# TensorE's program of 20 expert jobs written out in place of a loop over 10 pairs of jobs

## The chip, the cores and the metric

The kernel runs on one core of one Trainium2 chip. The metric is the device time of one execution in microseconds (us). Each engine of the core has a program of its own, and the engines keep in step by semaphores. PE is TensorE, DVE is VectorE, ACT is ScalarE, POOL is GpSimd, SP is SyncE, which here only issues transfers.

## The reference, cut to what matters

The reference is one transformer layer over 1024 tokens (32 sequences of 32) of width 512: cross attention, self attention, and then a mixture of experts with 8 experts, of which each token takes the best two:

```
logits = (x @ gate_w + gate_b) / TEMP
topk_vals, topk_idx = jax.lax.top_k(logits, TOP_K)
...
h = jnp.einsum('bsd,edf->bsef', x, w1) + b1
h = jax.nn.gelu(h, approximate=False)
expert_out = jnp.einsum('bsef,efd->bsed', h, w2) + b2
out = jnp.einsum('bse,bsed->bsd', gate_probs, expert_out)
```

followed by a layer norm and the residual. `w1` is 512 x 2048 and `w2` 2048 x 512 for each expert. The change lies in this last stage.

## The kernel before, in words

**Stages.** The first 780 us or so are the two attentions and the routing. The routing sorts the 2048 (token, expert) pairs by expert and cuts them into `JOBS` = 23 jobs of 128 rows each; a job belongs to one expert, and `job_e` holds each job's expert, which is known only at run time. From 786 us to 1303 us TensorE works on the jobs, and a short tail gathers the rows and normalizes them.

**A job on TensorE.** `job(j, turn)` (line 804) reads the job's expert `e` from memory into a register (`value_load`, line 805). Its work is in quarters of the 2048 hidden columns, `fb` = 0 to 3:

- `mm1(j, turn, fb, e)` (line 775): 48 matmuls of 128 columns in fp16, in 16 triples (lines 787, 788, 789). Numbers are kept as a high and a low half, so that a product takes three matmuls. The weights lie in one of two slots, chosen by `e % 2`; so the address of each piece of weights is worked out in a register, on TensorE's own sequencer, just before the instruction that uses it: two such steps a triple. These stay after the change, since `e` stays unknown.
- `mm2(j, fb)` (line 792): 12 matmuls of 512 columns (lines 799, 800, 801), with fixed addresses.
- `xt_fill(j + 1)` (line 765): four transposes (line 770) of the next job's rows.

They are interleaved as `mm1(j,0), mm2(j-1,2), mm1(j,1), xt_fill(j+1), mm2(j-1,3), mm1(j,2), mm2(j,0), mm1(j,3), mm2(j,1)`. Each `mm1` waits for a count of `h_act` (and the first for `xt_out` and `experts_in`), each `mm2` for `hT_out` and `v_low_done`, `xt_fill` for `xs_in` and `xt_out`. A count is a formula in `j`, such as

```
pe.wait_ge(hT_out, FB * j + fb + 1)
...
pe.wait_ge(v_low_done, 2 * (FB * j + fb + 1))
```

With `j` a Python number, that is a constant in the wait; with `j` a loop's register, it is worked out by a register step first.

**Loops.** Jobs 0, 1 and 22 are written out, in TensorE's program as in this text's diff. Jobs 2 to 21 are a hardware loop (`Fori`, line 828) of 10 passes over two jobs, since `turn` alternates. ACT and DVE run their own part of each job (gelu at line 490, the halves of `w2` at lines 506 and 647, the halves of the hidden rows at lines 498 and 638) in loops of their own; SP loads the next expert's 8 MB (lines 385 and 387) when `mm2_done` shows that a slot is free; POOL gathers rows and adds results (lines 433 and 438).

**Program code.** Each engine's instructions are fetched from the chip's memory by transfers that the profile lists under the kind "instruction", by queue.

Of the kernel before, what the change touches and what calls it, by code (L numbers as in the profile page):

```python
# [55 lines left out]
JOBS = TOKENS * TOPK // P + EXPERTS - 1  # L56
# [38 lines left out]
def perceiver_layer(nc, x, ctx_768, g_x, b_x, g_c, b_c, Wq, Wk, Wv, Wo, W_qkv, W_o,  # L95
                    gate_w, gate_b, w1, b1, w2, b2, ln_g, ln_b, out):
    with ExitStack() as stack:
# [666 lines left out]
        def moe_pe(pe):  # L764
            def xt_fill(j):
                pe.wait_ge(xs_in, 16 * (j + 1))
                if not isinstance(j, int) or j > 0:
                    pe.wait_ge(xt_out, j)
                for c in range(KD):
                    last = nc.tensor.transpose(XT[c], xs[:, c * P:(c + 1) * P], ident[:, :])  # L770
                    if c == 0 and isinstance(j, int) and j == 0:
                        last.then_inc(mm2_done, 1)
                last.then_inc(xt_full, 1)

            def mm1(j, turn, fb, e):
                if fb == 0:
                    pe.wait_ge(xt_out, j + 1)
                    pe.wait_ge(experts_in, e * 48 + 48)
                if not isinstance(j, int) or j > 0:
                    pe.wait_ge(h_act, FB * (j - 1) + fb + 1)  # L780
                elif fb == 2:
                    pe.wait_ge(b1_cols_ok, 1)
                for c in range(4):
                    into = bank[fb][:, c * P:(c + 1) * P]
                    for k in range(KD):
                        high, low = [moe_flat16[:, bass.ds((e % 2) * 32768 + (2 * k + i) * FF + fb * 512 + c * P, P)] for i in range(2)]
                        nc.tensor.matmul(into, high, xT_low[turn][:, k, :], start=(k == 0), stop=False)  # L787
                        nc.tensor.matmul(into, high, xT_high[turn][:, k, :], start=False, stop=False)  # L788
                        last = nc.tensor.matmul(into, low, xT_high[turn][:, k, :], start=False, stop=(k == KD - 1))  # L789
                last.then_inc(h_full, 1)  # L790

            def mm2(j, fb):
                pe.wait_ge(hT_out, FB * j + fb + 1)
                if fb == 0 and (not isinstance(j, int) or j > 0):
                    pe.wait_ge(ys_raw, j)
                pe.wait_ge(v_low_done, 2 * (FB * j + fb + 1))
                for c in range(4):
                    high, low = [v_place(part, j, fb, c // 2)[:, (c % 2) * DIM:(c % 2 + 1) * DIM] for part in range(2)]
                    nc.tensor.matmul(Y[:, :], hT_low[:, fb % 2, c, :], high, start=(fb == 0 and c == 0), stop=False)  # L799
                    nc.tensor.matmul(Y[:, :], hT_high[:, fb % 2, c, :], high, start=False, stop=False)  # L800
                    last = nc.tensor.matmul(Y[:, :], hT_high[:, fb % 2, c, :], low, start=False, stop=(fb == 3 and c == 3))  # L801
                last.then_inc(mm2_done, 1)

            def job(j, turn, first=False, last=False, behind=True):
                e = 0 if first else pe.value_load(job_e[0:1, bass.ds(j, 1)], min_val=0, max_val=EXPERTS - 1)
                mm1(j, turn, 0, e)
                if not first:
                    mm2(j - 1, 2 if behind else 3)
                mm1(j, turn, 1, e)
                if not first and not last:  # L810
                    xt_fill(j + 1)
                if behind:
                    mm2(j - 1, 3)
                mm1(j, turn, 2, e)
                mm2(j, 0)
                mm1(j, turn, 3, e)
                mm2(j, 1)
                if first:
                    xt_fill(j + 1)
                    mm2(j, 2)  # L820
# [4 lines left out]
            job(0, 0, first=True, behind=False)  # L825
            pe.wait_ge(jobs_ready, 1)
            job(1, 1, behind=False)
            with pe.Fori(2, JOBS - 1, 2) as j:
                job(j, 0)
                job(j + 1, 1)  # L830
            job(JOBS - 1, 0, last=True)
            mm2(JOBS - 1, 2)
            mm2(JOBS - 1, 3)
# [844 lines left out]
        def _(pe):  # L1678
# [347 lines left out]
            body(GROUPS - 1, True, True, False)  # L2026
            body(GROUPS, False, True, False)
            moe_pe(pe)


# [21 lines left out]
```

## Time and profile before

| what | value |
|---|---|
| median of 3 runs | 1328.2 us (1325.65 to 1328.8) |
| the profiled execution's own time | 1326.96 us |
| its span, first to last instruction | 1325.3 us |
| TensorE clock granted, mean | 0.993 |
| PE busy | 1277.7 us, 96% of the span |
| DVE busy | 971.1 us, 73% |
| ACT busy | 963.9 us, 73% |
| POOL busy | 219.1 us, 17% |

The busy time of PE overlaps itself, since matmuls are pipelined: a 128-column matmul is shown with 220 ns, while the next one starts 56 ns later. So the length of a stretch is read from the starts of its instructions, not from busy time. Register steps, branches and waits are run by an engine's sequencer and are not counted as busy; the view of a source line lists them under PEldq for TensorE.

### The profile page before, as it was taken

The page shows a single profiled execution, that of the slowest core. Times are in us where ns is not written, and L with a number is a line of the kernel's source. Part 1 is how long each engine was busy: PE and PEld are TensorE (multiplying, and loading weights), DVE is VectorE, ACT ScalarE, POOL GpSimd, SP SyncE. Part 2 cuts the span into 40 slices and gives each one's busy share as a digit, 9 for nine tenths or more (in the row PEclk, how much of TensorE's full clock was granted, in tenths as well). Part 3 has the DMA queues.
Part 4 walks back from the last instruction along what each step waited for, and adds up shares of the span by engine and source line. Part 5 has one row for each costly group of instructions (what it writes and reads, how often), then busy time and mean ns, then how long its engine had stood idle before and what let it go on. Part 6 is the DMA issues. An engine that isn't in the chain of part 4 may idle for free.

```text
span 1325.3 us, 34868 instructions
## 1 busy us (share of the span) xinstructions
PE 1277.7 (96%) x11476; PEld 952.9 (72%) x11477; DVE 971.1 (73%) x2140; ACT 963.9 (73%) x1741; POOL 219.1 (17%) x270
## 2 busy tenths in 40 slices
PE   7999999999999999999999789999999999999997
PEld 7768768677697696786876666777777777777773
DVE  5775878877877878788766757776767676767677
ACT  3577776776777777776877537787888888888784
POOL 1001002012030120030210213121212121111112
PEclk9999999999999999999999889999999999999999
DMA  9527246154363372552732895546262626710104
GB/s 365 191 101 255 90 159 223 63 209 169 99 252 122 110 250 87 182 198 68 255 146 90 317 344 166 222 168 201 95 214 80 228 79 229 277 32 16 32 9 135
DMA packets 69838, 216.36 MB, mean 163 GB/s; under 512 B 5582, under 2 KB 5820, under 8 KB 64652
## 3 DMA queue, kind: packets, MB, share of 16 engines
q1 hardware_dynamic: 63568, 201.71, 42.0%
q0 software_dynamic: 6192, 13.98, 5.1%
q8 instruction: 31, 0.51, 0.1%
q14 instruction: 19, 0.16, 0.0%
q10 hardware_dynamic: 28, 0.01, 0.0%
HBM read 169.46 MB, written 46.22 MB: 163 GB/s over the span
## 4 chain that ended last, share of the span: by engine, by line
PE 67%; DMA 9%; issue 8%; DVE 7%; ACT 4%; POOL 3%; SPq 1%; DVEq 0%; POOLq 0%; ACTq 0%
PE bank L799 7%; PE bank L1755 7%; PE bank L787 6%; PE bank L789 6%; PE bank L801 6%; PE bank L800 6%; PE bank L788 6%; DMA w_halves<-arena 4%; DMA w_halves<-moe_w 3%; PE bank L1804 3%; PE bank L1789 3%; PE bank L1821 3%; PE bank L1792 2%; PE bank L1764 2%; PE bank L1889 2%
## 5 line engine op out<-in xcount | busy, mean ns | idle before, releaser
L787 PE MATMUL bank<-arena,moe_w 128*128 128x128 f16 x1472 | 256.2, 220 | 0.9 <-DVE arena L630 0.9
L789 PE MATMUL bank<-arena,moe_w 128*128 128x128 f16 x1472 | 256.4, 220 | 0.0
L788 PE MATMUL bank<-arena,moe_w 128*128 128x128 f16 x1472 | 255.6, 219 | 0.0
L1755 PE MATMUL bank<-moe_w 128*128 128x257 f32 x768 | 188.6, 383 | 0.0
L787 PEld LDWEIGHTS bank<-arena,moe_w 128*128 (+1 forms) x1472 | 143.8, 98 | 14.9 <-DVE arena L630 1.2
L788 PEld LDWEIGHTS bank<-arena,moe_w 128*128 (+1 forms) x1472 | 144.1, 98 | 10.3
L1755 PEld LDWEIGHTS bank<-moe_w 128*128 128x128 f32 x768 | 137.9, 190 | 17.7
L789 PEld LDWEIGHTS bank<-arena,moe_w 128*128 (+1 forms) x1472 | 143.8, 98 | 1.5 <-issue 0.2
L490 ACT ACTIVATE arena<-bank,now_act 128x128 f32<-128x128 f32 x368 | 136.8, 449 | 7.9 <-PE bank L789 4.5
L506 ACT ACTIVATE wosT<-moe_w,now_act 128x1024 f16 (+1 forms) x90 | 98.5, 1143 | 37.7 <-PE bank L801 37.7
L1147 ACT ACTIVATE moe_w<-bank,cols,ugain 128x512 f32<-128x512 f32 x96 | 74.4, 776 | 59.7 <-PE bank L1805 58.7
L438 POOL DMA_INDIRECT acc_rows<-arena,job_idx x22 | 52.1, 2368 | 396.3 <-DVE arena L671 396.3
L1377 DVE TENSOR_TENSOR moe_w<-bank,moe_w 128x512 f16<-128x512 f32 (+1 forms) x96 | 65.4, 689 | 48.1 <-ACT moe_w L1161 45.8
L647 DVE SCALAR_TENSOR_TENSOR arena<-moe_w,now_v,wosT 128x1024 f16<-128x1024 f16 (+1 forms) x45 | 57.8, 1285 | 52.5 <-ACT wosT L506 50.3
L647 DVE SCALAR_TENSOR_TENSOR kqT<-moe_w,now_v,y 128x1024 f16<-128x1024 f16 (+1 forms) x45 | 57.8, 1285 | 51.3 <-ACT y L506 51.0
L1009 POOL TENSOR_TENSOR crstd<-cmv,half 128x3 f32<-128x3 f32 x32 | 28.7, 898 | 396.1 <-DVE cmv L1334 396.1
L1161 ACT CAST moe_w<-bank 128x512 f16<-128x512 f32 (+1 forms) x96 | 54.3, 585 | 47.2 <-PE bank L1779 46.9
L506 ACT ACTIVATE y<-moe_w,now_act 128x1024 f16 (+1 forms) x45 | 51.7, 1149 | 43.5 <-PE bank L801 43.5
L1789 PE MATMUL bank<-moe_w 128*128 128x512 f16 x192 | 73.0, 380 | 3.7 <-DVE moe_w L1377 1.8
L1792 PE MATMUL bank<-moe_w,arena 128*128 128x512 f16 x192 | 72.6, 378 | 0.0
L1140 ACT ACTIVATE moe_w<-bank,negm 128x257 f32<-128x257 f32 x128 | 59.0, 467 | 15.9 <-DVE negm L1357 15.3
L638 DVE SCALAR_TENSOR_TENSOR arena<-arena,now_h 128x512 f16<-128x512 f32 x92 | 68.7, 746 | 1.6 <-ACT arena L498 1.6
(296 smaller groups left out, 3099.3 us busy)
## 6 DMA issues: line engine op xcount, KB each, us to landing
moe_w<-in_L_ffn_w_dram SPq DMA_DIRECT2D x46, 1024.0 KB, 6.4
moe_w<-w_halves SPq DMA_DIRECT2D x8, 4096.0 KB
moe_w<-in_L_ffn_w_dram SPq DMA_DIRECT2D x8, 4096.0 KB
w_halves<-moe_w SPq DMA_DIRECT2D x48, 512.0 KB, 4.2
arena<-in_ctx_dram SPq DMA_DIRECT2D x32, 384.0 KB
arena<-in_L_ffn_w_dram SPq DMA_DIRECT2D x10, 1024.0 KB, 4.9
blocks<-in_L_ffn_w_dram SPq DMA_DIRECT2D x8, 1024.0 KB, 4.8
w_halves<-arena SPq DMA_DIRECT2D x8, 512.0 KB
```

The source lines that it names most:

```text
L490: last = nc.scalar.activation(h_sb[:, fb % 2, c * P:(c + 1) * P], bank[fb][:, c * P:(c + 1) * P], ACT.Gelu, bias=now_act[:, 4 + 4 * fb + c ...
L506: nc.scalar.activation(v_place(0, j, fb, i), moe_flat[:, bass.ds(slot * 16384 + 8192 + fb * 2048 + i * 1024, 1024)], ACT.Identity, scale=n ...
L647: nc.vector.scalar_tensor_tensor(out=v_place(1, j, fb, i), in0=moe_flat[:, bass.ds(slot * 16384 + 8192 + fb * 2048 + i * 1024, 1024)], sca ...
L787: nc.tensor.matmul(into, high, xT_low[turn][:, k, :], start=(k == 0), stop=False)
L788: nc.tensor.matmul(into, high, xT_high[turn][:, k, :], start=False, stop=False)
L789: last = nc.tensor.matmul(into, low, xT_high[turn][:, k, :], start=False, stop=(k == KD - 1))
L799: nc.tensor.matmul(Y[:, :], hT_low[:, fb % 2, c, :], high, start=(fb == 0 and c == 0), stop=False)
L800: nc.tensor.matmul(Y[:, :], hT_high[:, fb % 2, c, :], high, start=False, stop=False)
L801: last = nc.tensor.matmul(Y[:, :], hT_high[:, fb % 2, c, :], low, start=False, stop=(fb == 3 and c == 3))
L1755: last = nc.tensor.matmul(bank[h][:, 0:KEYS], qkT[:, c, b, h * P:(h + 1) * P], cnT[:, b % 2, c, :], start=(c == 0), stop=(c == KC - 1))
L1789: nc.tensor.matmul(ps[:, :], n_high[:, b % 2, k, columns], pT_high[:, k, :], start=(k == 0), stop=False)
L1792: nc.tensor.matmul(ps[:, :], n_low[:, b, k, columns], pT_high[:, k, :], start=False, stop=False)
```

## The change

The loop of TensorE's expert jobs becomes a Python loop, so that each of the jobs 2 to 21 is written out with its number as a constant. The order of the matmuls, their operands and all that is waited for stay. `turn` is `j % 2`, which is what the loop had. The programs of the other engines are not touched.

```
             job(1, 1, behind=False)
-            with pe.Fori(2, JOBS - 1, 2) as j:
-                job(j, 0)
-                job(j + 1, 1)
+            for j in range(2, JOBS - 1):
+                job(j, j % 2)
             job(JOBS - 1, 0, last=True)
```

So four things differ in TensorE's program: the branch at the end of each pass and its counter are gone; `value_load` has a fixed address; each wait's count is a constant in place of a register; and the code of the 20 jobs is ten times as long, each instruction run once.

## Rows read from the trace of the kernel before

**Rows 1.** The page: the busy time of each engine and its share of the span.
```profile
PE 1277.7 (96%) x11476; PEld 952.9 (72%) x11477; DVE 971.1 (73%) x2140; ACT 963.9 (73%) x1741; POOL 219.1 (17%) x270
```

**Rows 2.** The view of waits, 829 to 1276 us: total, times, longest.
```profile
ACT y L506 <- PE bank L801: 42.2, 40, 1.4
...
PEld bank L799 <- issue: 4.2, 20, 0.2
```

**Rows 3.** All engines over nine passes: length; PE, PEld, DVE, ACT, POOL busy; clock; DMA.
```profile
874.50:1276.61 402.11, 401.38 (x4394) 288.47 (x4393) 282.27 (x414) 326.04 (x594) 69.76 (x69) 1.00 0.40 130
```

**Rows 4.** The view of stretches, PE alone: window length, busy (instructions), PEclk, DMA share, GB/s.
```profile
829.06:1276.61 447.55, 446.48 (x4882) 1.00 0.43 139
...
829.06:851.88 22.82, 22.76 (x245) 1.00 0.45 175
851.88:874.50 22.62, 22.35 (x246) 1.00 0.79 256
874.50:897.07 22.57, 22.56 (x245) 1.00 0.43 169
897.07:919.11 22.04, 21.98 (x245) 1.00 0.82 268
...
1120.56:1142.67 22.11, 22.09 (x246) 1.00 0.45 176
...
1231.92:1254.51 22.59, 22.54 (x246) 1.00 0.14 23
1254.51:1274.01 19.50, 19.48 (x234) 1.00 0.10 13
1276.61:1295.63 19.02, 19.02 (x229) 1.00 0.11 16
```

**Rows 5.** Stretches, PE alone: single blocks of `mm1`, to the next block's start.
```profile
786.09:794.14 8.05, 8.05 (x144) 1.00 1.03 438
823.75:826.48 2.73, 2.73 (x50) 1.00 0.56 62
...
1231.92:1235.21 3.29, 3.29 (x50) 1.00 0.00 0
...
1243.64:1246.54 2.90, 2.85 (x50) 1.00 0.00 0
...
1287.46:1290.26 2.80, 2.80 (x49) 1.00 0.00 0
```

**Rows 6.** Weight loads in order of time, at the end of job 20's first `mm1`.
```profile
1234.34 0.10 PEld L787 LDWEIGHTS bank<-arena,moe_w 128*128 x1
...
1234.59 0.10 PEld L787 LDWEIGHTS bank<-arena,moe_w 128*128 x1
```

**Rows 7.** The view of source lines: TensorE's sequencer; ns min/median/max, first and last start.
```profile
L828 PEldq COMPARE_BRANCH  x10: 76/211/221, 872.1 to 1274.2; - x10
...
L793 PEldq ALU_OP  x80: 32/36/36, 832.2 to 1273.8; - x80
```

**Rows 8.** The view of the queues, from 829 to 874.5 us.
```profile
q8 instruction: 4, 0.07, 0.6%
```

**Rows 9.** The view of the queues, from 919 to 1274 us: two neighbouring lines.
```profile
q0 software_dynamic: 3504, 8.13, 12.5%
q14 instruction: 1, 0.01, 0.0%
```

**Rows 10.** The page: the code fetches of the whole span.
```profile
q8 instruction: 31, 0.51, 0.1%
```

**Rows 11.** Stretches, PE alone: one transpose fill and one `mm2`.
```profile
1262.71:1263.17 0.46, 0.46 (x5) 1.00 0.00 0
1263.17:1265.76 2.59, 2.59 (x14) 1.00 0.00 0
```

**Rows 12.** One expert's load: its issue, and the stretch in which its transfers end.
```profile
1087.31 0.33 SPq L385 DMA_DIRECT2D moe_w<-w_halves x1
...
1112.00:1117.00 5.00, 4.95 (x55) 3.37 (x53) 3.58 (x6) 3.70 (x8) 3.89 (x4) 1.00 0.37 64
```

## The prediction

> **What bounds the kernel now.** I read the page first, then the waits of the expert stage, then I cut that stage into jobs, a job into blocks, and looked at what TensorE's sequencer does at the seams. The page says that PE is busy 96% of the span [rows 1], which only tells where to look. The waits of 829 to 1276 us say more: ACT waits for PE some 40 times, 42.2 us in all, while PE itself waits only for "issue", 4.2 us in 20 gaps [rows 2]. "Issue" means that no semaphore of another engine was late; the instruction simply wasn't there. ACT and DVE are busy 326.0 and 282.3 of 402.1 us [rows 3], 81% and 70%. So TensorE sets the pace of the expert jobs, and where it idles, its own sequencer is late.
>
> The jobs themselves show how much. The 20 jobs in the loop take 447.55 us, from 829.06 to 1276.61, 22.38 a job [rows 4]. They are not alike. The first job of a pass takes 22.57 to 22.59 us, the second 22.04 to 22.11, again and again (two of each are among the rows, of nine passes); only the first pass is slower, with 22.82 and 22.62 [rows 4]. Two jobs of the same work, 0.5 us apart: that is the seam of the loop. And the granted clock is 1.00 in each of these stretches, the 2.4 GHz level, so the clock has no part in it.
>
> Where the 0.5 us goes is seen in the blocks. 144 matmuls of `mm1` in job 0, whose addresses are constants, take 8.05 us, so 48 of them take 2.68 at TensorE's own pace [rows 5]. A block with register addresses takes 2.73 to 2.90, and the first block behind the branch 3.29 [rows 5]. At the end of that slow block the weight loads come in a new rhythm: a triple begins at 1234.34 and the next at 1234.59, 0.25 us later, where TensorE needs 0.168 (2.68 / 16) [rows 5, 6]. That is the sequencer's pace through two register steps and three matmuls. During an `mm2` (12 matmuls, about 2.6 us) the sequencer runs ahead, during an `mm1` TensorE eats this lead, and each block of `mm1` ends just about as the lead runs out. So every register step near a seam is paid in full by TensorE, unless the lead still covers it. This is the whole lever of the change: it is about the sequencer, not about matmuls.
>
> **The change part by part.**
>
> *Branch and counter.* Each pass loses one COMPARE_BRANCH of 211 ns (median) [rows 7] and the two register steps of its counter. TensorE pays 22.59 - 22.11 = 0.48 us for it late in the stage and 22.57 - 22.04 = 0.53 in the second [rows 4]. Ten passes begin with such a job, the first one too, which has the loop's entry: 10 x 0.5 = 5.0 us saved.
>
> *Waits with constants.* Each `mm2` in the loop has an ALU step of 36 ns for its count (80 at line 793 for 20 jobs) [rows 7], and a second at line 796 for the other count. Written out they vanish. The nearest rows are blocks of the same place: `mm1` of quarter 2 ends after 2.90 us in job 20 and after 2.80 in job 22, which is already written out with constants [rows 5]. So constants are worth up to 0.1 us a block there, and less where the lead still covers them. From below they are worth nothing.
>
> *Code that streams.* In the loop TensorE's code is fetched once: the first pass has four fetches on q8, some 16 KB each [rows 8, 10], and in the eight passes from 919 to 1274 us q8 doesn't appear at all [rows 9]. Written out, each pair of jobs fetches as the first pass did, so that the page would show about 31 + 9 x 4 = 67 fetches on q8, about 1.1 MB, where it has 31 and 0.51 now [rows 10]. The bytes are nothing. What may cost is that the sequencer stumbles where new code comes in. The trace has a price for it from above: the second job of the first pass, which runs on new code with register waits, takes 22.62 against 22.04 for the same job one pass later [rows 4], 0.58 us more. It has one from below as well: job 22 runs on new code too, with constants. Without its fourth `mm2` and without a transpose fill it takes 19.02 us; the same seven blocks and a fill of job 21, in the loop, take 19.50 [rows 4]. The fill takes 0.46 us by the starts around it [rows 11], so job 21 without it is 19.04. New code with constants costs what old code with registers costs without a branch: the gain and the loss of these two parts cancel in job 22.
>
> The Trainium skill ("Runtime: NRT & Kernel Launch", section "Instruction fetch mechanics") says that the sequencer fetches its next pages by its own queue while it runs, mostly hidden, and that there is no instruction cache, so that a taken branch whose target isn't in the window forces a fetch. By that rule streaming costs next to nothing, the sum is that of the seams alone (5 us) or more, and each back edge has a fetch in it. This trace agrees with the first half only in part (job 3 pays 0.58 us) and doesn't show the second: there is no fetch on q8 through eight passes, so the loop's code stays where it is.
>
> *The sum.* I take job 22 as the model of a written-out job, as it is the only one that has both new code and constants and isn't held up by the start of the stage: 19.02 + 0.46 for the fill + 2.59 for the fourth `mm2` = 22.07 us [rows 4, 11]. 20 x 22.07 = 441.4, against 447.55: 6.15 us saved. The parts agree: 5.0 for ten seams, and 0.8 because the first pass is 0.78 slower than the second now (45.44 against 44.61) and is slower no more.
>
> *What could hide it.* Behind TensorE nothing else is close: ACT and DVE have 19% and 30% of idle time, and ACT's waits for PE show that they follow. The loads of experts must land before their first job. The one issued at 1087.3 us ends in the stretch of 1112 to 1117, where the DMA share is down to 0.37 [rows 12]: about 0.37 x 5 = 2 us into it, at 1114. Job 15, the first of that expert, begins only at 1120.56 [rows 4]. Some 6 us are left, and TensorE comes 0.6 us earlier over those two jobs. What comes behind, the last job, the gathers and the norm, starts when TensorE's last `mm2` ends and moves with it. So the saving reaches the end in full.
>
> The profiled execution took 1326.96 us, 1.7 more than its span. 1326.96 - 6.15 = 1320.8. The median is 1.2 above that execution, so against the median I expect 1328.2 - 6.2 = 1322.0. A change of 0.3% is 4.0 us, about what a measurement of this kernel can tell from none.
>
> **The rivals.**
>
> *Streaming costs what it did in the first pass: slower.* Then each job stays at 22.62 us, the pace of job 3 [rows 4], constants or not: 20 x 22.62 = 452.4, 4.9 us more than now, 1333.1. It would happen where a new page of code is opened while the lead is used up, worst while an expert's load fills the DMA engines (job 3 ran under a DMA share of 0.79). It decides from 22.38 us a job on, that is if new code costs TensorE more than 0.34 us above the 22.04 of a job without it. For it: job 3. Against it: job 3 pays also for its register waits, and job 22 and block 823.75 of job 1, 2.73 us with new code and constants [rows 5], do not show it.
>
> *Streaming costs only beside a load: no change that can be told.* Six experts are loaded during the loop, each in some 27 us (1087.3 to 1114) [rows 12], so 162 of the 447.55 us, or 7.2 jobs, have a load beside them. If these pay job 3's 22.62 and the other 12.8 job 22's 22.07, the sum is 445.4, 2.2 saved, 1326.0. For it: jobs 2 and 3 ran beside a load, job 22 didn't [rows 4]. Against it: as above, job 3 pays for its register waits too, and in these two jobs the whole surplus over job 22 is 0.55 to 0.75 us, of which the branch and the waits explain a part.
>
> *Constants give more.* If most blocks went at 2.73 us as the one in job 1, a job would be 4 x 2.73 + 4 x 2.59 + 0.46 = 21.74, and 20 of them 434.8: 12.7 us saved, 1315.5. The limit is at blocks of 2.68. Against it: job 22 has constants too, and its 19.02 us are three `mm2` of 2.59 and four blocks of 2.81 on average.
>
> *The branch costs nothing, the first job of a pass is slow for another reason.* Its value load is the same as in the second job, and its fetches are none; only the branch and its counter differ. I leave it almost no chance.
>
> **How the numbers follow.** The likeliest case, 22.0 to 22.18 a job, has 0.56: 4 to 7.5 us saved, 1320.7 to 1324.2. More from constants has 0.10, all of it faster. A price beside loads only has 0.25, within 0.3%. Streaming at job 3's price has 0.09, of which nearly all is slower. Faster by over 0.3%: 0.56 + 0.10 = 0.66; within: 0.26; slower: 0.08. The range leaves out the far ends of the two outer rivals: from 1318.5 (9.7 saved, between job 22's pace and job 1's) to 1327.0 (the price beside loads, and 1 us more).
>
> **What the changed profile would show.** COMPARE_BRANCH and line 828's steps are gone, and so are the ALU steps at 793. q8 has about 67 fetches. Even and odd jobs take the same time, 22.1 us, and no block of `mm1` reaches 3.1 us. Blocks with a page turn in them are 0.1 us longer than others; if they are 0.2 to 0.4 longer, and more so under a load, the first rival holds. "Issue" before line 799 stays, with shorter gaps. From the end of job 22's last `mm2` on, the tail is as long as before. I would be wrong at the root if TensorE began to wait for something else, a load or DVE, in the middle of the jobs.

## The result, and the profile after

The changed kernel takes 1317.13 us (median of 6 runs, 1314.98 to 1318.74), the kernel before beside it 1327.37 (6 runs, 1325.65 to 1328.8). The ratio is 0.9923, with a 95% interval of 0.9911 to 0.9934: 10.2 us saved, where 6.2 were forecast, and just below the range (1318.5). The forecast of 1322.0 started from a median of 1328.2, of three runs; with three more runs of the kernel before it is 1327.37, so 0.8 us of the distance between 1322.0 and 1317.13 lies in the starting point. The profiled execution took 1316.81 us.

The views of stretches, PE alone, with the columns of [rows 4]: the 20 jobs, then two of them, and then job 22 without its fill and fourth `mm2`, as the last row of [rows 4].

```profile
827.27:1266.43 439.16, 439.14 (x4882) 1.00 0.44 143
849.30:871.19 21.89, 21.89 (x245) 1.00 0.85 278
1222.43:1244.51 22.08, 22.08 (x246) 1.00 0.14 25
1266.43:1285.49 19.06, 19.06 (x229) 1.00 0.11 16
```

The 20 jobs take 439.16 us for 447.55 before, 8.4 less, 21.96 us a job. Even and odd jobs are alike now, between 21.86 and 22.08. Job 22, which was written out in both kernels, takes 19.06 for 19.02. From its first matmul to the end of the span it is 48.7 us in both. So the gain is in the jobs whose form changed, and it is 2.2 us more than forecast there.

TensorE's sequencer, by source line, and PE's gaps by the view of waits for the 20 jobs, answering to [rows 7] and [rows 2]; line 793 has no step any more, and line 828 no branch:

```profile
L796 PEldq EVENT_SEMAPHORE  x92: 51/51/51, 791.5 to 1289.7; - x92
```
```profile
ACT y L506 <- PE bank L801: 34.3, 40, 1.3
...
PEld bank L799 <- issue: 0.3, 2, 0.2
```

The "issue" gaps long enough to be counted fell from 20 (4.2 us) to 2 (0.3 us), and ACT still waits for PE. The page of the profile counts the code fetches, forecast at about 67 [rows 10]:

```profile
q8 instruction: 75, 1.23, 0.4%
```

The forecast counted four fetches for two jobs, as in the window of [rows 8]. There are 44 more than before for nine more pairs of jobs, 4.9 a pair. In the kernel before one more fetch begins at 917.83 us, in the second pass, between the windows of [rows 8] and [rows 9].

The view of source lines also gives the other steps of TensorE's sequencer, those beside the 128 address steps of a job. A job 4 to 21 has 10 of them in the changed kernel. In the kernel before, the second job of a pass has 17. The first has 21: three more for the counter and the branch, and two more for waits (lines 777 and 780), with one fewer for the value load.

Blocks of `mm1` now run from 2.68 to some 2.9 us, the first of a job too (four blocks of jobs 20 and 21, same view as [rows 5]):

```profile
1222.43:1225.33 2.90, 2.90 (x50) 1.00 0.00 0
1233.81:1236.50 2.69, 2.69 (x49) 1.00 0.00 0
1239.09:1241.92 2.83, 2.83 (x49) 1.00 0.76 104
1244.51:1247.19 2.68, 2.68 (x50) 1.00 0.00 0
```

No block reaches 3.1 us, as forecast. The forecast also gave a sign for costly new code, blocks 0.2 to 0.4 us longer where a new page of code comes in. It isn't there: blocks during which a fetch on q8 begins are 0.03 us longer on average than the others of the same quarter. What the profile alone doesn't tell is how the 8.4 us is made up, since three things changed at once: the branches, the waits, and where the code comes from.

### The profile page after: what moved, and what is told of

Its sections match the earlier page's. It is cut to its first block, busy times and chain, and to the rows that moved or that the text cites. A ratio compares the mean times of both kernels' runs of the same rounds, so it can differ in the third digit from the quotient of the medians.

```text
span 1315.2 us, 34686 instructions
## 1 busy us (share of the span) xinstructions
PE 1269.9 (97%) x11476; PEld 952.8 (72%) x11476; DVE 969.6 (74%) x2140; ACT 965.4 (73%) x1741; POOL 222.5 (17%) x270
## 4 chain that ended last, share of the span: by engine, by line
PE 67%; DMA 8%; issue 8%; DVE 7%; ACT 4%; POOL 3%; SPq 1%; DVEq 0%; POOLq 0%; ACTq 0%
PE bank L1754 7%; PE bank L787 6%; PE bank L799 6%; PE bank L789 6%; PE bank L800 6%; PE bank L801 6%; PE bank L788 6%; DMA w_halves<-arena 4%; DMA w_halves<-moe_w 3%; PE bank L1803 3%; PE bank L1788 3%; PE bank L1820 3%; PE bank L1791 2%; PE bank L1763 2%; PE bank L1888 2%
```

## The experiments

Two theories stood at the start. A: TensorE's sequencer has no lead left at the end of a block of `mm1`, so that each register step there is paid; constants in the waits are then a large part of the gain. B: the gain is the ten branches, and the rest is scatter. The ratios are to runs of the kernel before on the same chip; the median of these was between 1326.97 and 1328.33 us.

### e1: written out, but with register waits

```
-            for j in range(2, JOBS - 1):
-                job(j, j % 2)
+            with pe.Fori(0, 2, 2) as z:
+                for j in range(2, JOBS - 1):
+                    job(z + j, j % 2)
```

> The 20 jobs are written out as in the changed kernel, but inside a loop of a single pass whose register, always 0, is added to each job's number, so that every wait count and the address of the expert's number are worked out in registers again, as in the kernel before. One branch that is not taken, all code new. Theory A (constants in the waits are a large part of the gain: TensorE's sequencer has no lead left when a block of mm1 ends, so each register step there is paid): a job takes 22.3 to 22.6 us, as in the first pass of the kernel before (22.62), where the changed kernel has 21.96; 7 to 13 us slower than the changed kernel, so 1324 to 1330. Theory B (the gain is the ten branches, the rest is scatter of the attention stage): 21.96 us a job and 1317 as the changed kernel.

1330.21 us, ratio 1.0010 (1.0001 to 1.0020): a hair slower than the loop, and 13 us slower than the changed kernel. Its 20 jobs, and the one branch of its wrapping loop:

```profile
830.36:1281.34 450.98, 448.49 (x4882) 1.00 0.43 140
853.22:875.83 22.61, 22.34 (x245) 1.00 0.78 257
943.54:965.92 22.38, 22.29 (x246) 1.00 0.46 180
```
```profile
L828 PEldq COMPARE_BRANCH  x1: 83/83/83, 1278.9 to 1278.9; - x1
L793 PEldq ALU_OP  x80: 32/36/36, 833.5 to 1278.5; - x80
```

22.55 us a job: close to the pace of job 3 before (22.62), kept up over all 20 jobs. B falls. Writing the jobs out and keeping register waits loses 3.4 us against the loop (450.98 against 447.55), although ten seams are gone.

The sequencer's steps make two clean comparisons. A job of e1 has the same 17 steps beside the address steps as the second job of a pass in the loop. The second jobs of passes 2 to 10 take 22.08 us on average, and jobs 4 to 21 of e1 take 22.53: new code costs 0.45 us a job with these waits. The changed kernel has seven steps fewer than e1, mostly register steps for wait counts, and one for the address of the value load. They are worth 450.98 - 439.16 = 11.8 us, 0.59 a job. The durations that the records give them add up to only 0.2 us a job; why they cost more was not taken apart, nor was what it is in new code that slows the sequencer.

One other cause can be ruled out from the trace. In e1 the view of waits puts 12 gaps, 2.3 us, down to DVE's line 647, as in

```profile
PEld bank L799 <- DVE arena L647: 1.2, 6, 0.3
```

But the halves that each `mm2` waits for had ended at least 2.4 us before it began, in every job: TensorE was not waiting for DVE there.

### e2: four jobs a pass, in the loop

```
-            for j in range(2, JOBS - 1):
-                job(j, j % 2)
+            with pe.Fori(2, JOBS - 4, 4) as j:
+                for i in range(4):
+                    job(j + i, i % 2)
```

> The loop of the kernel before with four jobs a pass, five passes: half as many branches, register waits as before, and a body twice as long (some 160 KB by the fetches of the first pass, 4 of 16 KB for two jobs). Theory A: if the longer body still stays in place, half of the seams are gone and a job takes 22.04 + 0.5/4 = 22.2 us, 1324; if it is fetched anew in each pass, q8 shows over 65 fetches as in the changed kernel (75), all code is new with register waits, 22.5 us or more a job, and the change of place at each back edge costs at least its 1 us of fetch: 1330 to 1340. Theory B: only the number of branches counts, 2.5 us less than before, 1325, whatever q8 shows.

1350.38 us, ratio 1.0170 (1.0156 to 1.0184). The page of the profile has 80 fetches on q8, so the longer body doesn't stay. The first form of theory A falls, and B too; the second form holds, and was too cheap. Line 828, then stretches of PE around the first back edge (the branch back to the top of the body): the last `mm2` of job 5 with the idle time behind it, the first `mm1` of job 6, and more. The same two stretches at the second and at the third back edge follow, and then the timeline at the first:

```profile
L828 PEldq COMPARE_BRANCH  x5: 83/3724/5902, 913.6 to 1292.9; - x5
```
```profile
913.46:918.61 5.15, 2.76 (x12) 1.00 0.14 43
918.61:923.40 4.79, 4.79 (x48) 0.64 0.00 0
923.40:926.00 2.60, 2.60 (x16) 1.00 0.00 0
1007.75:1012.95 5.20, 2.76 (x15) 1.00 0.14 50
1012.95:1017.26 4.31, 4.31 (x49) 1.00 0.00 0
1101.71:1109.15 7.44, 2.76 (x14) 0.90 0.93 320
1109.15:1114.24 5.09, 5.09 (x48) 0.50 1.04 394
```
```profile
918.61 0.23 PE L787 MATMUL bank<-arena,moe_w 128*128 128x128 f16 x1 [2.39 <-issue]
```

The branch takes 3.7 us in the median and 5.9 at worst, where it takes 0.211 with two jobs a pass [rows 7]. Within each of the four taken branches one code fetch of 16 KB begins on q8. TensorE idles for 2.39, 2.44, 4.69 and 2.49 us. The first block behind it takes 4.79, 4.31, 5.09 and 4.32 us, where e1's first blocks take 2.99 on average. Most of that is the missing lead and not the clock: behind the second and the fourth back edge the granted clock is 1.00, and the block still takes 4.3 us, near the sequencer's own 16 x 0.25 = 4.0. Behind the first and the third the clock is granted at 0.64 and 0.50, part or all of the block at the lower level, 1.2 GHz, and this adds some 0.5 and 0.8 us. Together the 20 jobs take 469.76 us, 18.8 more than e1, 4.7 a back edge. The profiled execution, 1345.86 us, was the fastest of the five; the others took 1350.0 to 1351.1 us at a mean granted clock of 0.985 to 0.988, where it had 0.992.

### e3 and e4: the same extra work at two places

A second load of the expert's number, its value unused, at the head of each job (e3), or between `mm2(j,0)` and the last `mm1` (e4):

```
+                if not first:
+                    pe.value_load(job_e[0:1, bass.ds(j, 1)], min_val=0, max_val=EXPERTS - 1)
```

> The changed kernel with the expert's number read a second time at the head of each job (jobs 1 to 22), value unused: some 0.6 us more work for TensorE's sequencer (a load of 0.30 us and its register steps) at the place where the loop's branch was, and no work for any other engine. Theory A: at the head of a job the first load has used up the sequencer's lead, so TensorE pays nearly all of it: 0.4 to 0.6 us a job, the first block of mm1 3.2 to 3.4 us, 1326 to 1330. Rival C (the sequencer hides such work anywhere, the branch was dear for its fetch or for being taken): no change, 1317.

> The same second load, but between mm2(j,0) and the last mm1 of the job, where no other load is. Theory A: an mm2 of 2.6 us gives the sequencer about 1 us of free time before the next mm1 begins, so the same 0.6 us costs 0 to 0.15 us a job: 1317 to 1320, and the last mm1 of a job stays under 2.95 us. Rival C: as at the head, whatever that is. A rival to A (the sequencer is short of time all over, lead or not): 0.4 to 0.6 us a job here as well, 1326 to 1330.

e3: 1329.89 us, ratio 1.0022 (1.0013 to 1.0032). e4: 1316.61 us, ratio 0.9920 (0.9906 to 0.9933), the same as the changed kernel. The load, its place in e3 (line 806), and the 20 jobs and one first `mm1` of e3:

```profile
L806 PEldq TENSOR_LOAD <-job_e x22: 297/303/483, 804.3 to 1277.9; - x22
L806 PEldq FUSED_REGOPS  x22: 151/151/165, 804.8 to 1278.3; - x22
```
```profile
829.05:1280.42 451.37, 451.26 (x4882) 1.00 0.43 140
1190.25:1212.80 22.55, 22.55 (x246) 1.00 0.14 25
1190.25:1193.58 3.33, 3.33 (x49) 1.00 0.00 0
```

The 20 jobs of e4:

```profile
826.63:1266.19 439.56, 439.56 (x4882) 1.00 0.44 143
```

One and the same 0.6 us of sequencer work costs TensorE 0.61 us a job at the head, (451.37 - 439.16) / 20, and 0.02 between `mm2(j,0)` and the last `mm1`. Theory A comes out about as forecast, at its upper end, and rival C falls. At the head the job's own load has used up the free time of one `mm2`; at e4's place this time is unused. The old branch stood at the dearer of the two places.

### e5: constant addresses

```
-                        high, low = [moe_flat16[:, bass.ds((e % 2) * 32768 + ...
+                        high, low = [moe_flat16[:, bass.ds((expert_of[j] % 2) * 32768 + ...
```

> The changed kernel with constant addresses for the weights of mm1 in jobs 1 to 22: the slot of each job is written into the program from the list of experts that these inputs give, so the program holds for these inputs only. The expert's number is still loaded and still used for the wait on experts_in. Both register steps of each triple vanish. Theory A (what is left of TensorE's idle time is its sequencer's lead running out through these steps): each mm1 takes 2.68 us as in job 0, a job 4 x 2.68 + 4 x 2.59 + 0.46 = 21.54 against 21.96, 8 to 9 us less than the changed kernel: 1308. Rival D (ACT or DVE is next, hidden until now): blocks of mm1 still at 2.68, but mm2 begins late, on DVE; 1312 or more. Rival E (the idle time at the end of a block is the change from 128 to 512 columns, or new code, not the steps): 1316.

The slot of each job is a constant taken from these inputs' routing, so this is a bound, not a kernel to use. 1307.14 us, ratio 0.9852 (0.9829 to 0.9874).

```profile
826.98:1257.42 430.44, 430.44 (x4881) 1.00 0.45 146
998.96:1020.48 21.52, 21.52 (x246) 1.00 0.44 173
```

Every job takes 21.52 us, each block of `mm1` 2.68: TensorE's own pace, on new code in every job. So all that the changed kernel still loses in these jobs, 0.44 us each, goes with the address steps: without them the sequencer's lead doesn't run out. New code costs nothing here. It is shorter code, though, with 39 fetches on q8 during the 20 jobs for 49 in e1. Rivals D and E fall.

### e6: the load moved away from the head

```
-                e = 0 if first else pe.value_load(job_e[0:1, bass.ds(j, 1)], min_val=0, max_val=EXPERTS - 1)
+                e = 0 if first else loaded[0] if early and j > 2 else expert_now(j)
...
                 mm2(j, 0)
+                if early and 2 <= j < JOBS - 1:
+                    loaded[0] = expert_now(j + 1)
                 mm1(j, turn, 3, e)
```

> The changed kernel with the expert's number of job j + 1 read in job j, between mm2(j,0) and the last mm1, where a second load was free (e4), and not at the head of job j + 1, where a second one cost 0.61 us. Theory A: the head's single load fills the sequencer's free time nearly to the brim, so taking it away gives the first block of mm1 at most what it lacks, some 0.1 us a job: 0 to 2 us less than the changed kernel, 1315 to 1317, first blocks at 2.7 to 2.8 like the others. If the head's load were paid in part already, 0.3 us or more a job, 1311 or less.

1318.4 us, ratio 0.9942 (0.9925 to 0.9958); the 20 jobs take 438.83 us, 0.3 less than in the changed kernel. The jobs come out at the low end of the forecast of 0 to 2 us, while the median lies above the 1315 to 1317 us that were expected. There is nothing to be had: first blocks take 2.80 us on average with the load moved and 2.79 with it at the head, so one load there just fits.

### e7: a quarter of `mm2` inside each `mm1`

In three of the four pairs of a job, three matmuls of `mm2` go ahead of the last quarter of `mm1`, in jobs 2 to 21:

```
+            def mixed(j, turn, fb, e, jj, ff):
+                mm1(j, turn, fb, e, between=lambda cs: mm2(jj, ff, cs))
+                mm2(jj, ff, range(1, 4))
...
                 for c in range(4):
+                    if between is not None and c == 3:
+                        between(range(0, 1))
```

> The changed kernel with a quarter of mm2 (three matmuls of 512 columns) moved ahead of the last quarter of the mm1 before it, for three of the four pairs of a job; addresses stay in registers. Same work. Theory A: the three long matmuls give the sequencer 0.65 us with little to do in the middle of a block, so the lead doesn't run out: the pairs take 5.28 instead of 5.37, 0.25 to 0.3 us a job less, 5 to 6 us in all, 1311 to 1312. Rival D: mm2 now begins 0.65 us sooner and mm1 ends 0.65 us later, 1.3 us off the slack of DVE's halves of the hidden rows (2.3 us at the tightest); if the slack is less than it looks, TensorE waits for DVE and it is 1317 or more.

1311.0 us, ratio 0.9884 (0.9865 to 0.9903). The 20 jobs, and one mixed pair: 36 matmuls, 3, 12 and 9:

```profile
828.82:1261.82 433.00, 433.00 (x4882) 1.00 0.44 145
975.10:977.11 2.01, 2.01 (x38) 1.00 0.64 57
977.11:977.76 0.65, 0.65 (x7) 1.00 1.05 192
977.76:978.43 0.67, 0.67 (x14) 1.00 0.57 83
978.43:980.37 1.94, 1.94 (x13) 1.00 0.40 127
```

The pair takes 5.27 us, TensorE's own pace, with all address steps in place. 6.2 us are saved in the jobs, where 5 to 6 were forecast.

### e8, e9, e10: the fourth pair, and the loop

e8 mixes the pair around the transpose fill as well; e9 is e8 in the loop of the kernel before, e10 is e7 in that loop.

```
-                mm1(j, turn, 1, e)
+                mm1(j, turn, 1, e, between=lambda cs: mm2(j - 1, 3, cs))
                 xt_fill(j + 1)
-                mm2(j - 1, 3)
+                mm2(j - 1, 3, range(1, 4))
```

> e7 with the fourth pair of each job mixed in the same way (the last quarter of mm1(j,1) behind the first three matmuls of mm2(j-1,3)). Theory A: that pair falls from about 2.76 to 2.68 as well, so 0.05 to 0.1 us a job less than e7's 21.65: the 20 jobs 431 to 432 us, 1309 to 1310.

> e8's order of matmuls in the loop of the kernel before: ten taken branches, register waits, code that stays in place. Theory A (branches, register waits and new code all cost only where the sequencer's lead runs out): the mixing gives back the lead in the middle of each block, so the register waits are hidden, the first block of a pass pays a part of its 0.5 us, and the 20 jobs take 432 to 436 us, less than the 439 of the changed kernel although nothing is written out: 1311 to 1314. If branch and register waits cost TensorE as before whatever the order, 439 to 440 us and 1318 or more.

e8: 1314.83 us, ratio 0.9899 (0.9883 to 0.9914). e9: 1323.04 us, ratio 0.9967 (0.9955 to 0.9979). Both expectations missed: the jobs take 436.00 and 442.95 us, where 431 to 432 and 432 to 436 were expected. The fourth pair did fall to TensorE's pace, but the block after it, the 36 matmuls before `mm2(j,0)`, grew. It is shown here for e8, with the same block of another quarter for comparison, then DVE's work just before, in order of time:

```profile
973.90:976.23 2.33, 2.17 (x37) 1.00 1.08 394
968.18:970.19 2.01, 2.01 (x37) 1.00 1.02 392
```
```profile
973.76 1.13 DVE L630 SCALAR_TENSOR_TENSOR arena<-bank,now_scales,arena 128x128 f16<-128x128 f32 x4 [0.71 <-ACT arena L482]
975.38 0.75 DVE L656 SCALAR_TENSOR_TENSOR arena<-bank,now_y,blocks 128x512 f32<-128x512 f32 x1 [0.49 <-issue]
```

The first matmul of `mm2(j,0)` comes at 976.23, 0.10 us after line 656, `y_copy`, has ended at 976.13. It empties the bank that `mm2(j,0)` starts to fill. This distance is 0.10 us in each of the jobs 3 to 21 of e8, where it is 0.32 to 0.60 in e7 and 1.02 to 1.37 in the changed kernel: in e8 the matmul always waits for it. DVE does it behind the halves of the next job's rows (line 630), and these wait for the fill, which e8 had moved 0.65 us back. In e8 the view of waits calls this gap "issue"; in e9 it names the wait, 20 times:

```profile
PE bank L802 <- DVE arena L656: 5.4, 20, 0.3
```

So this was a new wait, on a chain from job to job whose slack e7 had already cut to less than half and which had not been worked out. e10 was made to take it away.

> e7's order (three pairs of four mixed, the pair beside the transpose fill not) in the loop of the kernel before. In e8 and e9 TensorE waited once a job for DVE's copy of Y (line 656), 0.35 to 0.5 us, since the fill had moved behind the first three matmuls; e7 had no such wait, so it should be gone here. Theory A: register waits are hidden in the mixed blocks, code stays in place, and only the first block of a pass pays for the branch, 0.36 us as in e9: 20 x 21.6 + 10 x 0.36 = 435.6 us (434.5 to 437), 1313 to 1315, below the changed kernel's 1317 with nothing written out. If it comes to 438 us or more, the branch or the register waits cost more than e9's blocks show, or DVE's copy is late again.

e10: 1316.58 us, ratio 0.9928 (0.9909 to 0.9947). The 20 jobs, a pass's first block of 36 matmuls behind the branch, and another:

```profile
828.88:1265.59 436.71, 436.71 (x4882) 1.00 0.43 143
916.32:918.70 2.38, 2.38 (x38) 1.00 0.00 0
905.78:907.79 2.01, 2.01 (x37) 1.00 1.05 385
```

436.71 us lies within the bounds forecast (434.5 to 437), the median 1.6 us above those for the whole (1313 to 1315). Register waits are hidden: the second jobs of the passes take 21.64 us on average, e7's jobs 21.65. The branch still costs 0.37 us in each first block. The whole gain of the change is had without writing anything out, with 31 code fetches on q8 as before; e7 beats e10 by the ten branches, 3.7 us.

### The changed kernel again

> The changed kernel once more, unchanged. In the first pair of profiles 8.4 of the 10.1 us lie in the 20 jobs and 1.6 ahead of the expert stage, where nothing is changed. If that 1.6 us is scatter, the first mm1 begins somewhere in 783 to 788 us this time, the 20 jobs take 439.2 us (within 0.5) again, and the median stays within 1.5 us of 1317. If something systematic shortens the attention stage, it begins at 784.5 again.

1316.56 us, ratio 0.9929 (0.9912 to 0.9946). The 20 jobs:

```profile
825.51:1264.66 439.15, 439.10 (x4881) 1.00 0.44 143
```

439.15 for 439.16: the sum of the jobs repeats to 0.01 us. The first `mm1` begins at 784.73, after 784.47 in the first profile; in the other profiles, whose attention stage is the same, it lies between 783.96 (e4) and 789.62 (e8). So the 1.6 us ahead of the jobs is no more than scatter between profiles can make.

## Why the prediction was wrong in size and right in direction

**What bounds the kernel.** Right. TensorE sets the pace, and where it idles its sequencer is late. e5 shows it from one side (no address steps, 2.68 us a block), e3 from the other (0.6 us more at the head, 0.61 us paid). "Every register step near a seam is paid in full by TensorE, unless the lead still covers it" is what e3 and e4 measured. One reading was too broad: that "only the first pass is slower". Job 6, the first of the third pass, takes 22.84 us, with a first block of 3.56:

```profile
919.11:941.95 22.84, 22.79 (x245) 1.00 0.13 23
919.11:922.67 3.56, 3.56 (x49) 1.00 0.00 0
```

The fetch of 917.83 begins 1.3 us before it. Whether it is the cause no run shows.

**Ten seams, 5.0 us.** Right as far as the runs tell. Over passes 2 to 10 the first job takes 22.60 us and the second 22.08 on average, so a seam is 0.52. It holds two more register steps for waits beside the branch and its counter, which the prediction left out; "only the branch and its counter differ" was not so. e10's seam costs 0.37 us in a mixed block, where part of the lead is given back. In the old order no run took the branch alone away.

**Code that streams, and waits with constants.** This is the step that failed, by its size: "the gain and the loss of these two parts cancel in job 22", and so "I take job 22 as the model of a written-out job". Both parts are larger than the prediction held for likely, and they don't cancel. Against the loop's second job, 22.08 us, new code costs 0.45 us (e1) and the constants give back 0.57 over the same jobs 4 to 21 (0.59 over all 20), which leaves 21.96 us a job and not 22.07. The 20 jobs take 439.16 us for the 441.4 forecast, 2.2 us less, and that is the whole error of the sum itself. "Up to 0.1 us a block" for the constants was right for the changed kernel against the loop, where it is 0.09 in the blocks of quarter 2; it was no measure of the constants themselves, since new code was mixed in. (The check "the parts agree" has a slip: 45.44 - 44.61 is 0.83, not 0.78.)

Job 22 was too small a sample. Its code is the same in ten of the profiles (all but those of e3, e4 and e5), and it takes from 18.88 to 19.39 us in them, a spread of 0.5 us that the model multiplied by 20. In the changed kernel it takes 19.06, where an average job has 21.96 - 2.59 - 0.46 = 18.91. The prediction had the bounds at hand (block 823.75 of job 1, 2.73 us) and put a chance of 0.10 on them.

**The rest of the 10.2 us.** 8.4 are in the jobs, and 8.4 by itself would have been inside the range (up to 9.7 saved). What carried the time past its edge is the 0.8 us of the starting point, and 1.8 to 2.0 us of the medians' difference that are not in the jobs, in both sets of runs, with nothing in the prediction for them. The intervals (8.8 to 11.8 us saved, and 7.2 to 11.7) are wide enough for most of it to be scatter. Against that stands this: subtracting each kernel's 20 jobs from its median gives 879.8 to 880.6 us for the four kernels with a loop of taken branches (before, e2, e9, e10), and 876.7 to 879.6 for the eight written out. In the profiled executions alone the two groups overlap, 876.1 to 879.7 us and 875.8 to 882.6. So a part may be the program's own, but no run shows it, and the cause stays open.

**What could hide it.** Right: neither loads nor DVE nor ACT took the place of the sequencer, even at e5's pace. But the claim held for this order only: e8 found DVE's copy of Y as soon as the fill moved by 0.65 us.

**The rivals.** Streaming at job 3's price was true of written-out code with register waits (22.55 us a job in e1) and false of the change, since the constants are worth more than it. Streaming only beside a load falls: jobs with and without a load beside them differ by no more than the scatter (21.89 at a DMA share of 0.85, 22.08 at 0.14), and in e1 job 6 takes 22.67 us at a share of 0.13, while jobs 11 and 16 take 22.46 and 22.44 at 0.80. "Constants give more" was the right one, to two thirds of its 12.7 us.

**The rule on branches and fetches.** By the Trainium skill ("Runtime: NRT & Kernel Launch", section "Instruction fetch mechanics") a taken branch forces a fetch unless its target is in the current window of two pages, each of 16 KiB. With four jobs a pass the runs agree: a fetch begins within each taken branch, which takes 3.7 us in the median. With two jobs they don't: the body is about five fetches of 16 KB long, more than two pages, and after the second pass no fetch is seen [rows 9]. So the stretch of code that stays is longer here than that window. In the same section the Trainium skill gives TensorE 128 KiB of instruction memory, and with this the trace agrees: five fetches of 16 KB fit, the body of four jobs, twice as long, doesn't. No run shows where between two and four jobs a body stops staying. The Trainium skill says in the same section that crossing a page boundary is mostly hidden. That holds in e5, where every job takes 21.52 us, and not in e1, where new code costs 0.45 us a job.

## What to carry to other kernels

Where TensorE idles for "issue", count register steps, and where they stand: the same 0.6 us of sequencer work cost 0.61 us at a job's head and 0.02 us behind another `mm2`. Here writing the loop out paid through its constants; with register waits kept it lost 3.4 us. Before writing out, try to put long matmuls between the short ones that need register addresses: it gave as much in the loop (1316.6 us) as writing out (1316.6 to 1317.1), and both together 1311.0. And don't let one written-out sample stand for twenty when the whole gain is a few tenths of a microsecond a sample.

## What the runs showed of the hardware that was not expected

- A taken branch took 0.211 us in the median with a body of two jobs (about five code fetches, once), and 3.7 us in the median, 5.9 at most, with four jobs, when the body was fetched anew in each pass and a fetch began within each branch (e2).
- After idle time at such a branch TensorE's clock fell in two cases of four: it was granted at 0.64 over the next 4.79 us after 2.39 us, at 0.50 over the next 5.09 us after 4.69 us, and at 1.00 after 2.44 and 2.49 us. What decides is not shown. PE's idle gaps of at most 0.3 us in the jobs of the other kernels left it at 1.00.
- Behind a branch that leaves the sequencer no lead, a block of 48 matmuls took 4.3 us at a clock of 1.00, where it takes 2.68 without address steps (e2, e5).
- New code slowed a sequencer that has no lead: 0.45 us a job in e1, with 49 fetches during the 20 jobs. It cost nothing in e5, with 39 fetches and no address steps.
